# Feed-forward of a two-layer kernel: how many up products go with one step of the sigmoid pass, and where the up half is rounded first

## The chip, the cores and the metric

The kernel runs on one core of a Trainium2 chip. The metric is the time of one execution on the device in microseconds (us), taken as the median of several runs; lower is better. The engines are called as in the profile: PE (TensorE, matrix products), DVE (VectorE), ACT (ScalarE), POOL (GpSimd) and SP (SyncE, which here only issues DMAs). Each runs its own instructions strictly in the order in which they were written, and they wait for one another through semaphores.

## The reference, cut to what matters

4096 tokens of width 256 go through two mixture-of-experts layers, an attention and a feed-forward. The change touches the last one alone:

```python
x    = act_qdq(layernorm(x))                    # act_qdq: round to 16 bits with ONE scale for
up   = act_qdq(x @ lpbq_dequant(w_up).T)        # the whole tensor, scale = max|x| / 32767
gate = act_qdq(x @ lpbq_dequant(w_gate).T)
sig  = fixed_qdq_u16(jax.nn.sigmoid(gate))
gate = act_qdq(gate * sig)
o    = act_qdq(gate * up)
return o @ lpbq_dequant(w_down).T               # added to x
```

`gate`, `up` and `o` are 4096 x 768. Every `act_qdq` needs the largest absolute value of the whole tensor before the first element can be rounded, so each is a barrier between two passes over the data.

## The kernel before, in words

In `gated_ffn` the 4096 x 768 values of `gate` stay in SBUF (`act_all`, 128 partitions x 24,576 floats). `up` has no room there: it is made in 48 products of 128 x 512 (`NP` = 48), copied out of PSUM into one of four buffers `u_out` (`UB` = 4), and stored to the DRAM tensor `up_raw`. Later it is loaded back in 12 pieces of 128 x 2048 floats, 1 MB each, into `later`, which has four places (`LB` = 4) and lies in the memory of `yT`, the transposed input of the up products. So no piece can be loaded before the last up product.

Three stages matter here.

**Sigmoid pass**, 24 steps (`STEPS`) of 1024 columns. For step i, ACT rounds the gate values of step i+1 (`round_gate`, L1672), takes the sigmoid of step i (`sigmoid`, L1678) and copies two up products out of PSUM (`evict_up`, L1640). DVE makes the sigmoid's integers (`sigmoid_integers`, L1827), takes the largest gated value of the step before (`gated_max`, L1836), multiplies gate and sigmoid (`gated`, L1831), and takes the largest value of the same two up products (L1845). PE makes the up products; product n waits until product n-4 has left its bank. `evict_up(n)` waits for product n, for the store and the maximum of n-4 (its buffer). `sigmoid(i)` waits for `gated(i-4)`. SP issues the 48 stores (L1503), waits for all of them, and then issues the loads of the pieces (L1510).

**Two scales.** When the pass is over DVE reduces the 48 maxima of up (L1847), POOL reduces them over the partitions (L1528), and DVE computes the scale of up (`new_scale`, L1772 to L1777; semaphore `s_scale` becomes 3). The scale of the gated values follows in the same way (L1853; `s_scale` 4).

**Wide pass**, 12 pieces (`WIDE`). ACT rounds piece i of up in its place in `later` (`round_up`, L1691, waits for the load of piece i) and piece i of the gated values (`round_gated`, L1695). DVE multiplies the two (L1866) and takes the largest value of the product of the piece before (L1861). SP issues the load of piece i only when `s_o["product"]` has reached i-3, that is after the DVE product of piece i-4, which reads the same place:

```python
free(sp, s_o["product"], i - LB + 1)
sp.dma_start(later[:, i % LB, :], up_raw[:, i * CW:(i + 1) * CW]).then_inc(s_later[i % LB], 16)
```

The order of the instructions on each engine is the order of the Python loops; nothing reorders it. After the wide pass comes the down projection, which the change does not touch.

Of the kernel before, what the change touches and what calls it, by code (L numbers as in the profile page):

```python
# [9 lines left out]
ALU = mybir.AluOpType  # L10
ACT = mybir.ActivationFunctionType
AX_X = mybir.AxisListType.X
# [1352 lines left out]
def low16(ap):  # L1365

    return ap.bitcast(I16).rearrange("p (n two) -> p n two", two=2)[:, :, 0]


def gated_ffn(nc, name, x_all, stats, act_all, I, w_up, w_down, up_raw, out):  # L1370
# [16 lines left out]
    WIDE = COLS // CW  # L1387
    NP = TG * IC
    BANKS = 4
    UB = 4  # L1390
    PAIRS = T // 2
    SIG_ROUND = 192.0
    SIG_TOP = 65535.0 / 65536.0

    with ExitStack() as ctx:
        sem = ctx.enter_context(stage_semaphores(nc, name))

        def sb(n, shape, dt):
            return ctx.enter_context(nc.sbuf_tensor(f"{name}_{n}", shape, dt))
# [16 lines left out]
        round_c = sb("round_c", [P, 1], F32)  # L1416
# [8 lines left out]
        maxes = sb("maxes", [P, 2, NP], F32)  # L1425
        step_max = sb("step_max", [P, T], F32)
        largest = sb("largest", [P, 5], F32)
        reduced = sb("reduced", [P, 5], F32)

        scale = sb("scale", [P, 5], F32)  # L1430
        to_int = sb("to_int", [P, 5], F32)
        tmp = sb("tmp", [P, 5], F32)
        unit = sb("unit", [P, 3], F32)
        u_all = sb("u_all", [P, UB, N], F32)
        u_out = [u_all[:, p, :] for p in range(UB)]
        work = sb("work", [P, 4, CB], F32)
# [6 lines left out]
        later = yT[:].rearrange("p h c t -> p (h c t)").bitcast(F32).rearrange("p (n c) -> p n c", c=CW)  # L1443
        LB = 4
# [8 lines left out]
        s_big = sem("largest_ready"); s_red = sem("largest_reduced"); s_scale = sem("scales_ready")  # L1453
        s_t = sem("x_rounded"); s_qt = sem("x_transposed"); s_qh = sem("yT_hi_ready"); s_ql = sem("yT_lo_ready")
        s_pr = sem("product_in_bank"); s_ev = sem("bank_copied"); s_um = sem("up_max_taken")
        s_us = [sem(f"up{i}_stored") for i in range(UB)]
        s_g = {k: sem("gate_" + k) for k in ("rounded", "sigmoid", "sig", "product", "max")}
        s_later = [sem(f"later{i}_loaded") for i in range(LB)]
        s_o = {k: sem("o_" + k) for k in ("up_rounded", "rounded", "product")}
# [5 lines left out]
        BIG_X, BIG_GATE, BIG_UP, BIG_GATED, BIG_O = range(5)  # L1465
# [14 lines left out]

        def gate_at(g, c):
            return flat[:, g * GW + c * N:g * GW + (c + 1) * N]

        def step(i):
            return flat[:, i * CB:(i + 1) * CB]
# [12 lines left out]
        def _(sp):  # L1498
            sp.dma_start(w_in[1].rearrange("p (c d) -> p c d", d=D), w_up.rearrange("(c p) d -> p c d", p=P)).then_inc(s_w[1], 16)
            sp.dma_start(w_in[2].rearrange("p (c i) -> p c i", i=I), w_down.rearrange("(c p) i -> p c i", p=P)).then_inc(s_w[2], 16)  # L1500
            for n in range(NP):
                sp.wait_ge(s_ev, NP + n + 1)
                sp.dma_start(up_raw[:, n * N:(n + 1) * N], u_out[n % UB]).then_inc(s_us[n % UB], 16)  # L1503
            for b in range(UB):
                sp.wait_ge(s_us[b], 16 * (NP // UB))
            sp.wait_ge(s_pr, 2 * NP)
# [4 lines left out]
            out_pairs = out.rearrange("(q k p) d -> q p k d", k=2, p=P)  # L1511
            for q in range(PAIRS):
                sp.wait_ge(s_d["out"], q + 1)
                sp.dma_start(out_pairs[q], u_out[q % 2].rearrange("p (k d) -> p k d", k=2)).then_inc(s_out[q % 2], 16)
            for p in range(2):
                sp.wait_ge(s_out[p], 16 * PAIRS // 2)

# [14 lines left out]
        def _(pe):  # L1532
# [25 lines left out]
            def product(i, g, c0):  # L1558

                n = i * NP + g * IC + c0  # L1560
                if n >= BANKS:
                    pe.wait_ge(s_ev, n - BANKS + 1)
                y_at_g = [y[:, :, g * N:(g + 1) * N] for y in (yT_hi, yT_lo)]
                bank = ps[4 + n % BANKS][:]
                for c in range(DC):
                    hi, lo = (w[:, i, c, c0 * P:(c0 + 1) * P] for w in (guT_hi, guT_lo))
                    nc.tensor.matmul(bank, hi, y_at_g[0][:, c], start=(c == 0), stop=False)  # L1567
                    nc.tensor.matmul(bank, hi, y_at_g[1][:, c], start=False, stop=False)  # L1568
                    mm = nc.tensor.matmul(bank, lo, y_at_g[0][:, c], start=False, stop=(c == DC - 1))  # L1569
                mm.then_inc(s_pr, 1)  # L1570
# [15 lines left out]
            for g in range(TG):  # L1586
                for c0 in range(IC):
                    product(1, g, c0)
            for q in range(PAIRS):
                pe.wait_ge(s_d["lo"], q + 1)  # L1590
# [14 lines left out]
        def _(act):  # L1605
            A = nc.scalar
# [22 lines left out]
            def evict_gate(g, c0):  # L1629
                n = g * IC + c0  # L1630
                act.wait_ge(s_pr, n + 1)
                A.activation(gate_at(g, c0), ps[4 + n % BANKS][:], ACT.Copy).then_inc(s_ev, 1)

            def evict_up(n):
                act.wait_ge(s_pr, NP + n + 1)

                if n >= UB:
                    act.wait_ge(s_us[n % UB], 16 * (n // UB))
                    act.wait_ge(s_um, n - UB + 1)
                A.activation(u_out[n % UB], ps[4 + (NP + n) % BANKS][:], ACT.Copy).then_inc(s_ev, 1)  # L1640
# [13 lines left out]
            for g in range(TG):  # L1654
# [3 lines left out]
                for c0 in range(IC):  # L1658

                    if c0 == 0 and (g + 1) * GW > y_at and g * GW <= y_at + T * D:  # L1660
                        act.wait_ge(s_qt, min(PAIRS, 2 * g + 2))
                    evict_gate(g, c0)
# [8 lines left out]
            def round_gate(i):  # L1671
                A.activation(step(i), step(i), ACT.Identity, bias=round_c[:], scale=to_int[:, 1:2]).then_inc(s_g["rounded"], 1)  # L1672

            def sigmoid(i):
                act.wait_ge(s_g["rounded"], i + 1)
                if i >= SB:
                    act.wait_ge(s_g["product"], i - SB + 1)
                A.activation(sig[i % SB], low16(step(i)), ACT.Sigmoid, scale=scale[:, 1:2]).then_inc(s_g["sigmoid"], 1)  # L1678

            act.wait_ge(s_scale, 2)  # L1680
            round_gate(0)
            for i in range(STEPS):
                if i + 1 < STEPS:
                    round_gate(i + 1)
                sigmoid(i)
                for n in (2 * i, 2 * i + 1):
                    evict_up(n)

            def round_up(i):
                act.wait_ge(s_later[i % LB], 16 * (i // LB + 1))  # L1690
                A.activation(later[:, i % LB, :], later[:, i % LB, :], ACT.Identity, bias=round_c[:],  # L1691
                             scale=to_int[:, 2:3]).then_inc(s_o["up_rounded"], 1)

            def round_gated(i):
                A.activation(wide_step(i), wide_step(i), ACT.Identity, bias=round_c[:], scale=to_int[:, 3:4]).then_inc(s_o["rounded"], 1)  # L1695

            act.wait_ge(s_scale, 3)
            round_up(0)
            act.wait_ge(s_scale, 4)
            for i in range(WIDE):  # L1700
                round_gated(i)
                if i + 1 < WIDE:
                    round_up(i + 1)

            def round_product(q):

                if q >= 2:
                    act.wait_ge(s_d["lo"], q - 1)
                A.activation(wide[q % 2][:, 0:GW // 2].rearrange("p (c t) -> p c t", c=IC), pair_of_tiles(q),  # L1709
                             ACT.Identity, bias=round_c[:], scale=to_int[:, 4:5]).then_inc(s_d["rounded"], 1)  # L1710
# [9 lines left out]
            round_product(0)  # L1720
            for q in range(PAIRS):
                if q + 1 < PAIRS:
                    round_product(q + 1)
# [3 lines left out]
        def _(dve):  # L1727
            V = nc.vector
# [38 lines left out]
            def new_scale(c, unit):  # L1767


                big = reduced[:, c:c + 1]  # L1770
                if unit is not None:
                    order(V.tensor_scalar(tmp[:, c:c + 1], big, unit, None, ALU.mult))  # L1772
                    big = tmp[:, c:c + 1]
                order(V.tensor_scalar(scale[:, c:c + 1], big, 1 / QMAX, 1e-12, ALU.mult, ALU.max))
                order(V.reciprocal(to_int[:, c:c + 1], scale[:, c:c + 1]))
                if unit is not None:
                    order(V.tensor_scalar(to_int[:, c:c + 1], to_int[:, c:c + 1], unit, None, ALU.mult))  # L1777
# [28 lines left out]
            for g in range(TG):  # L1806
                for c0 in range(IC):
                    n = g * IC + c0
# [29 lines left out]
            for i in range(STEPS):  # L1838
                sigmoid_integers(i)
                if i > 0:  # L1840
                    gated_max(i - 1)
                gated(i)
                for n in (2 * i, 2 * i + 1):
                    dve.wait_ge(s_ev, NP + n + 1)
                    V.tensor_reduce(maxes[:, 1, n:n + 1], u_out[n % UB], AX_X, ALU.max, apply_absolute_value=True).then_inc(s_um, 1)  # L1845
            dve.wait_ge(s_um, NP)
            V.tensor_reduce(largest[:, BIG_UP:BIG_UP + 1], maxes[:, 1, :], AX_X, ALU.max).then_inc(s_big, 1)  # L1847
            gated_max(STEPS - 1)
            dve.wait_ge(s_red, 3)
            new_scale(2, unit[:, 0:1])  # L1850
            V.nop().then_inc(s_scale, 1)
            dve.wait_ge(s_g["max"], STEPS)
            V.tensor_reduce(largest[:, BIG_GATED:BIG_GATED + 1], step_max[:, 0:STEPS], AX_X, ALU.max).then_inc(s_big, 1)  # L1853
            dve.wait_ge(s_red, 4)
# [94 lines left out]
```

## Time and profile before

| | us |
|---|---|
| median of 3 runs (1688.80 to 1694.94) | 1692.29 |
| the profiled execution | 1692.64 |
| its span in the trace | 1690.9 |
| sigmoid pass, 1445.2 to 1542.9 | 97.7 |
| two scales, 1542.9 to 1548.0 | 5.1 |
| wide pass, 1548.0 to 1602.5 | 54.5 |
| down projection, 1602.5 to 1690.9 | 88.4 |

The span is what the trace covers; the profiled execution took 1.7 us more around it. Busy times of engines are not additive: the engines work beside one another. What bounds a stage is read from the engine that is never idle in it, and from what the others wait for.

### The profile page before, as it was taken

Reading aid. Unit: us, or ns where it says so; the run is one execution under the profiler, and the core shown is the slowest. Engines: PE = TensorE matmul, PEld = TensorE weight load, DVE = VectorE, ACT = ScalarE, POOL = GpSimd, SP = SyncE. Lnnn points to the kernel's source line nnn. Section 1 sums busy time; section 2 is a strip of 40 time slices with the busy share of each in tenths; the row PEclk is TensorE's granted clock in tenths of the full one; section 3 lists DMA queues with packets and bytes.
Section 4 is the critical chain, followed back from the end, with each engine's and each line's share of the span. In section 5 each row is a group of like instructions: output and inputs, shape, how many; then the busy total and the mean of one; then the engine's idle time right before and its main releaser. Section 6 shows DMA issues by size and latency. Waiting matters only on the chain. (4 is left out here: it accounts for less than half of the span.)

```text
span 1690.9 us, 31990 instructions
## 1 busy us (share of the span) xinstructions
PE 1317.8 (78%) x10558; PEld 1070.7 (63%) x10559; DVE 1198.5 (71%) x2040; ACT 832.3 (49%) x1240; POOL 523.8 (31%) x592
## 2 busy tenths in 40 slices
PE   6169999999999428999438898999998589761077
PEld 3159788888898217889426787878887545320066
DVE  3869766655565386976248888888888677898944
ACT  3447333333332225633116555555655456886764
POOL 0055666655653114565312223322224100000000
PEclk9579999999999668999758988888889589996599
DMA  9557433333232545732250000000000100336311
GB/s 326 157 155 223 98 51 54 50 50 47 47 48 26 184 136 168 227 60 43 28 169 11 10 10 9 9 9 9 9 9 4 38 1 1 125 124 225 122 45 57
DMA packets 103445, 134.31 MB, mean 79 GB/s; under 512 B 16192, under 2 KB 87488, under 8 KB 101568
## 3 DMA queue, kind: packets, MB, share of 16 engines
q1 hardware_dynamic: 81856, 103.33, 18.6%
q0 software_dynamic: 21504, 29.83, 10.8%
q8 instruction: 55, 0.90, 0.2%
q14 instruction: 30, 0.25, 0.0%
HBM read 88.43 MB, written 44.70 MB: 79 GB/s over the span
## 5 line engine op out<-in xcount | busy, mean ns | idle before, releaser
L600 ACT ACTIVATE top_x_all<-top_h_ps,top_b1T 128x256 f32<-128x256 f32 x448 | 186.3, 473 | 324.0 <-PE top_h_ps L480 278.5
L478 PE MATMUL top_h_ps<-top_xT_hi,top_w_hi 128*128 128x256 f16 x896 | 247.6, 276 | 1.9 <-DVE top_xT_lo L779 1.0
L479 PE MATMUL top_h_ps<-top_xT_lo,top_w_hi 128*128 128x256 f16 x896 | 247.6, 276 | 0.0
L480 PE MATMUL top_h_ps<-top_xT_hi,top_w_lo 128*128 128x256 f16 x896 | 247.4, 276 | 0.0
L496 PE MATMUL top_y_ps<-top_w_hi,top_x_all 128*128 x896 | 245.0, 273 | 0.1
L497 PE MATMUL top_y_ps<-top_w_lo,top_x_all 128*128 x896 | 244.9, 273 | 0.0
L498 PE MATMUL top_y_ps<-top_w_hi,top_x_all 128*128 x896 | 244.7, 273 | 0.0
L358 POOL DMA_INDIRECT x_sum<-top_x_all,top_rows_out x112 | 186.4, 1664 | 126.0 <-POOL top_rows_out L354 73.0
L790 DVE CAST top_x_all<-top_x_all 128x512 f16<-128x512 f32 x224 | 101.1, 451 | 150.9 <-ACT top_x_all L600 138.6
L792 DVE TENSOR_TENSOR top_x_all<-top_x_all 128x512 f16<-128x512 f32 x224 | 155.7, 695 | 7.7
L346 POOL DMA_INDIRECT top_xg<-normed,top_rows_in x112 | 123.2, 1100 | 90.1 <-POOL top_rows_in L343 81.7
L343 POOL COPY top_rows_in<-top_row_of_slot 128x1 int32<-128x1 int32 (+1 forms) x112 | 95.5, 852 | 133.2 <-DVE top_row_of_slot L769 133.0
L1113 PEld LDWEIGHTS attn_out_ps<-attn_v,attn_probT 128*128 128x128 f32 x1024 | 129.8, 202 | 4.7 <-issue 0.3
L1012 POOL TENSOR_TENSOR attn_q_parts<-attn_q,attn_q_parts 128x512 f16<-128x512 f32 x32 | 37.1, 1160 | 305.1 <-ACT attn_q_parts L1176 305.1
L1113 PE MATMUL attn_out_ps<-attn_v,attn_probT 128*128 128x17 f32 x1024 | 127.8, 267 | 0.0
L1599 PE MATMUL ffn_ps<-ffn_dT_hi,ffn_yT 128*128 128x256 f16 x192 | 53.1, 277 | 91.9 <-DVE ffn_yT L1879 91.9
L1103 PE MATMUL attn_S<-attn_ident,attn_prob 128*128 128x128 f32 x512 | 87.2, 325 | 37.1 <-ACT attn_prob L1192 37.0
L1196 ACT ACTIVATE attn_probT<-attn_S 128x1024 f32<-128x1024 f32 x64 | 65.5, 1024 | 83.4 <-PE attn_S L1103 83.4
L1311 DVE COPY_PREDICATED attn_S<-attn_masked,attn_tiny 128x1024 f32<-128x1024 int32 x64 | 103.5, 1617 | 1.7 <-PE attn_S L1097 1.6
L478 PEld LDWEIGHTS top_h_ps<-top_xT_hi,top_w_hi 128*128 x896 | 88.9, 99 | 13.3 <-issue 2.7
L1103 PEld LDWEIGHTS attn_S<-attn_ident,attn_prob 128*128 128x128 f32 x512 | 67.6, 163 | 46.4 <-ACT attn_prob L1192 43.3
L480 PEld LDWEIGHTS top_h_ps<-top_xT_hi,top_w_lo 128*128 x896 | 88.9, 99 | 11.3
(297 smaller groups left out, 3152.6 us busy)
## 6 DMA issues: line engine op xcount, KB each, us to landing
top_staged<-in_L_xattn_W SPq DMA_DIRECT2D x32, 512.0 KB
top_staged<-in_L_ffn_w SPq DMA_DIRECT2D x32, 512.0 KB
up_raw<-ffn_u_all SPq DMA_DIRECT2D x48, 256.0 KB, 2.1
ffn_yT<-up_raw SPq DMA_DIRECT2D x12, 1024.0 KB, 4.8
normed<-top_x_all SPq DMA_DIRECT2D x2, 4096.0 KB, 14.1
top_w_lo<-in_ctx SPq DMA_DIRECT2D x4, 1024.0 KB, 9.9
top_x_all<-in_x SPq DMA_DIRECT2D x4, 1024.0 KB, 11.8
x_sum<-top_x_all SPq DMA_DIRECT2D x4, 1024.0 KB, 11.1
```

What stands on the lines that cost most here:

```text
L346: nc.gpsimd.indirect_dma_start(out=xg[i][:, k, :], out_offset=None, in_=normed, in_offset=bass.IndirectOffsetOnAxis(ap=rows[:, 0:1], axis= ...
L358: nc.gpsimd.indirect_dma_start(out=x_sum, out_offset=bass.IndirectOffsetOnAxis(ap=rows_out[k][:, 0:1], axis=0), in_=y[p][:, k, :], in_offs ...
L478: nc.tensor.matmul(out, hi, xT_hi[p][:, c, :], start=(c == 0), stop=False)
L479: nc.tensor.matmul(out, hi, xT_lo[p][:, c, :], start=False, stop=False)
L480: last = nc.tensor.matmul(out, lo, xT_hi[p][:, c, :], start=False, stop=(c == DC - 1))
L496: nc.tensor.matmul(out, h_hi[p][:, fc, rows], hi, start=(fc == 0 and k == 0), stop=False, skip_group_check=True)
L497: nc.tensor.matmul(out, h_hi[p][:, fc, rows], lo, start=False, stop=False, skip_group_check=True)
L498: last = nc.tensor.matmul(out, h_lo[p][:, fc, rows], hi, start=False, stop=(fc == FC - 1), skip_group_check=True)
L600: last = nc.scalar.activation(h32[:, fc * R:(fc + 1) * R], h_ps[:, b, q * R:(q + 1) * R], ACT.Relu, bias=b1T[:, bass.ds(e * FC + fc, 1)], ...
L792: V.tensor_tensor(lo, part, hi, ALU.subtract).then_inc(s_hl[p], 1)
L1103: mm = nc.tensor.transpose(S[:, r, c, :], prob[:, r * HC + c, :], ident[:])
L1113: mm = nc.tensor.matmul(out_ps[:, h * V1:(h + 1) * V1], probT[:, h, :], v32[i][:, 2 * c + r, :], start=True, stop=True)
```

## The change

Three things are moved; no operation is added or taken away.

1. Three up products go with each of the first 16 steps of the sigmoid pass (`UP_STEPS` = 16) instead of two with each of the 24, on ACT and on DVE.
2. The reduction of up's maxima stands on DVE in step 16 and its scale in step 17.
3. ACT rounds the first four pieces of up (`round_up(0)` to `round_up(3)`) inside steps 19 to 22 of the sigmoid pass. In the wide pass `round_gated(i)` is then followed by `round_up(i + 4)` where it was followed by `round_up(i + 1)`.

SP's code is the same: 48 stores, then 12 loads with the same waits.

```diff
+    UP_A_STEP = 3
+    UP_STEPS = NP // UP_A_STEP
+    UP_EARLY = (UP_STEPS + 3, UP_STEPS + 4, UP_STEPS + 5, UP_STEPS + 6)
...
+        def ups(i):
+            return range(UP_A_STEP * i, min(NP, UP_A_STEP * (i + 1)))
...
             for i in range(STEPS):
                 if i + 1 < STEPS:
                     round_gate(i + 1)
                 sigmoid(i)
-                for n in (2 * i, 2 * i + 1):
+                for n in ups(i):
                     evict_up(n)
+                if i in UP_EARLY:
+                    act.wait_ge(s_scale, 3)
+                    round_up(i - UP_EARLY[0])
...
-            act.wait_ge(s_scale, 3)
-            round_up(0)
             act.wait_ge(s_scale, 4)
             for i in range(WIDE):
                 round_gated(i)
-                if i + 1 < WIDE:
-                    round_up(i + 1)
+                if i + LB < WIDE:
+                    round_up(i + LB)
...
                 gated(i)
-                for n in (2 * i, 2 * i + 1):
+                if i == UP_STEPS:
+                    dve.wait_ge(s_um, NP)
+                    V.tensor_reduce(largest[:, BIG_UP:BIG_UP + 1], maxes[:, 1, :], AX_X, ALU.max).then_inc(s_big, 1)
+                if i == UP_STEPS + 1:
+                    dve.wait_ge(s_red, 3)
+                    new_scale(2, unit[:, 0:1])
+                    V.nop().then_inc(s_scale, 1)
+                for n in ups(i):
...
-            dve.wait_ge(s_um, NP)
-            V.tensor_reduce(largest[:, BIG_UP:BIG_UP + 1], maxes[:, 1, :], AX_X, ALU.max).then_inc(s_big, 1)
             gated_max(STEPS - 1)
-            dve.wait_ge(s_red, 3)
-            new_scale(2, unit[:, 0:1])
-            V.nop().then_inc(s_scale, 1)
```

ACT's rows around the end of the sigmoid pass before the change (a row is a line of the program, the operation, what it writes and reads; L1678 is the sigmoid of the last steps, L1691 rounds a piece of up in the place of `yT`, L1695 a piece of the gated values):

```order
L1678 ACTIVATE ffn_work<-ffn_act_all,ffn_scale 128x1024
L1640 ACTIVATE ffn_u_all<-ffn_ps 128x512 x2
L1691 ACTIVATE ffn_yT<-ffn_yT,ffn_round_c,ffn_to_int 128x2048
L1695 ACTIVATE ffn_act_all<-ffn_act_all,ffn_round_c,ffn_to_int 128x2048
L1691 ACTIVATE ffn_yT<-ffn_yT,ffn_round_c,ffn_to_int 128x2048
L1695 ACTIVATE ffn_act_all<-ffn_act_all,ffn_round_c,ffn_to_int 128x2048
```

The same place after it, from step 22 on (L1678 is now `round_gate`, L1684 the sigmoid, L1688 rounds a piece of up, L1704 a piece of the gated values):

```order
L1678 ACTIVATE ffn_act_all<-ffn_act_all,ffn_round_c,ffn_to_int 128x1024
L1684 ACTIVATE ffn_work<-ffn_act_all,ffn_scale 128x1024
L1688 ACTIVATE ffn_yT<-ffn_yT,ffn_round_c,ffn_to_int 128x2048
L1684 ACTIVATE ffn_work<-ffn_act_all,ffn_scale 128x1024
L1704 ACTIVATE ffn_act_all<-ffn_act_all,ffn_round_c,ffn_to_int 128x2048
L1688 ACTIVATE ffn_yT<-ffn_yT,ffn_round_c,ffn_to_int 128x2048
L1704 ACTIVATE ffn_act_all<-ffn_act_all,ffn_round_c,ffn_to_int 128x2048
```

The kinds alternate in the wide pass as before, but the L1688 behind the first L1704 is now piece 4, where it was piece 1.

DVE's rows in steps 17 and 18 after the change (L1834, L1843 and L1838 are the three instructions of a step, L1779 to L1784 the scale of up):

```order
L1838 TENSOR_TENSOR ffn_act_all<-ffn_act_all,ffn_work 128x1024
L1779 TENSOR_SCALAR ffn_tmp<-ffn_reduced,ffn_unit 128x1
L1781 TENSOR_SCALAR ffn_scale<-ffn_tmp 128x1
L1782 RECIPROCAL ffn_to_int<-ffn_scale 128x1
L1784 TENSOR_SCALAR ffn_to_int<-ffn_to_int,ffn_unit 128x1
L1834 TENSOR_SCALAR ffn_work<-ffn_work 128x1024
```

The scale of up has moved in front of step 18; from there on a step has no maxima of up.

## Rows read from the trace of the kernel before

**Rows 1.** The page's first line.

```profile
span 1690.9 us, 31990 instructions
```

**Rows 2.** Busy time by stretch (count), then granted clock, DMA share, GB/s.

```profile
core 0: us, PE busy (x) PEld busy (x) DVE busy (x) ACT busy (x) POOL busy (x), PEclk, DMA share, GB/s
1445.20:1542.90 97.70, 60.80 (x264) 24.03 (x264) 97.54 (x122) 75.92 (x93) 0.35 (x1) 0.94 0.41 151
1548.00:1602.50 54.50, 0.00 (x0) 0.00 (x0) 52.88 (x24) 43.57 (x22) 0.00 (x0) 0.50 0.45 154
```

**Rows 3.** Groups by line, 1440 to 1545: busy, mean ns, idle before, releaser.

```profile
L1567 PE MATMUL ffn_ps<-ffn_yT,ffn_guT_hi 128*128 128x512 f16 x94 | 35.9, 381 | 23.3 <-ACT ffn_u_all L1640 23.3
L1640 ACT ACTIVATE ffn_u_all<-ffn_ps 128x512 f32<-128x512 f32 x48 | 28.0, 601 | 13.1 <-DVE ffn_maxes L1845 13.1
```

**Rows 4.** Timeline of DVE, one step: start, duration.

```profile
1533.41 0.68 DVE L1827 TENSOR_SCALAR ffn_work<-ffn_work 128x1024 f32<-128x1024 f32 x1
1534.01 1.21 DVE L1836 TENSOR_REDUCE ffn_step_max<-ffn_act_all 128x1 f32<-128x1024 f32 x1
1535.14 1.22 DVE L1831 TENSOR_TENSOR ffn_act_all<-ffn_act_all,ffn_work 128x1024 f32<-128x1024 int16 x1
1536.27 1.27 DVE L1845 TENSOR_REDUCE ffn_maxes<-ffn_u_all 128x1 f32<-128x512 f32 x2
1537.46 0.68 DVE L1827 TENSOR_SCALAR ffn_work<-ffn_work 128x1024 f32<-128x1024 f32 x1
```

**Rows 5.** Timeline of ACT, one step, with the idle time before.

```profile
1492.51 1.19 ACT L1640 ACTIVATE ffn_u_all<-ffn_ps 128x512 f32<-128x512 f32 x2 [0.69 <-DVE ffn_maxes L1845]
1493.60 1.23 ACT L1672 ACTIVATE ffn_act_all<-ffn_act_all,ffn_round_c,ffn_to_int 128x1024 f32<-128x1024 f32 x1
1494.73 1.14 ACT L1678 ACTIVATE ffn_work<-ffn_act_all,ffn_scale 128x1024 f32<-128x1024 int16 x1
```

**Rows 6.** Timeline of PE, two matmuls of an up product in a row.

```profile
1527.30 0.38 PE L1569 MATMUL ffn_ps<-ffn_yT,ffn_guT_lo 128*128 128x512 f16 x1
1527.52 0.38 PE L1567 MATMUL ffn_ps<-ffn_yT,ffn_guT_hi 128*128 128x512 f16 x1
```

**Rows 7.** Timeline of DVE, the two scales.

```profile
1542.87 0.20 DVE L1772 TENSOR_SCALAR ffn_tmp<-ffn_reduced,ffn_unit 128x1 f32<-128x1 f32 x1
...
1543.86 0.18 DVE L1853 TENSOR_REDUCE ffn_largest<-ffn_step_max 128x1 f32<-128x24 f32 x1
...
1545.15 0.21 DVE L1777 TENSOR_SCALAR ffn_to_int<-ffn_to_int,ffn_unit 128x1 f32<-128x1 f32 x1
```

**Rows 8.** Timeline of ACT, start of the wide pass.

```profile
1545.80 2.08 ACT L1695 ACTIVATE ffn_act_all<-ffn_act_all,ffn_round_c,ffn_to_int 128x2048 f32<-128x2048 f32 x1
1547.79 2.08 ACT L1691 ACTIVATE ffn_yT<-ffn_yT,ffn_round_c,ffn_to_int 128x2048 f32<-128x2048 f32 x1
1549.77 2.08 ACT L1695 ACTIVATE ffn_act_all<-ffn_act_all,ffn_round_c,ffn_to_int 128x2048 f32<-128x2048 f32 x1
```

**Rows 9.** Timeline of DVE, start and end of the wide pass.

```profile
1547.98 2.29 DVE L1866 TENSOR_TENSOR ffn_act_all<-ffn_act_all,ffn_yT 128x2048 f32<-128x2048 int16 x1 [2.31 <-ACT ffn_act_all L1695]
1551.88 2.29 DVE L1866 TENSOR_TENSOR ffn_act_all<-ffn_act_all,ffn_yT 128x2048 f32<-128x2048 int16 x1 [1.61 <-ACT ffn_act_all L1695]
1554.09 2.28 DVE L1861 TENSOR_REDUCE ffn_step_max<-ffn_act_all 128x1 f32<-128x2048 f32 x1
...
1598.04 4.47 DVE L1861 TENSOR_REDUCE ffn_step_max<-ffn_act_all 128x1 f32<-128x2048 f32 x2
```

**Rows 10.** The loads: one issue, SP's waits for DVE, and time to landing.

```profile
1550.30 0.32 SPq L1510 DMA_DIRECT2D ffn_yT<-up_raw  x1
...
SPq L1510 <- DVE ffn_act_all L1866: 39.8, 8, 11.8
...
DMA to landing us min/median/max: 4.7/4.8/11.4
```

**Rows 11.** Busy time by stretch, while the first four loads run together.

```profile
1539.00:1543.00 4.00, 0.00 (x0) 0.00 (x0) 3.96 (x7) 0.00 (x0) 0.35 (x1) 0.50 1.01 426
```

More of the change, by code:

```diff
@@ L1678, in sigmoid, with round_up @@
                 A.activation(sig[i % SB], low16(step(i)), ACT.Sigmoid, scale=scale[:, 1:2]).then_inc(s_g["sigmoid"], 1)
+            def round_up(i):
+                act.wait_ge(s_later[i % LB], 16 * (i // LB + 1))
+                A.activation(later[:, i % LB, :], later[:, i % LB, :], ACT.Identity, bias=round_c[:],
+                             scale=to_int[:, 2:3]).then_inc(s_o["up_rounded"], 1)
             act.wait_ge(s_scale, 2)
@@ L1685, in _ @@
                 sigmoid(i)
-                for n in (2 * i, 2 * i + 1):
+                for n in ups(i):
                     evict_up(n)
[L1689 to L1692, printed above, removed]
+                if i in UP_EARLY:
+                    act.wait_ge(s_scale, 3)
+                    round_up(i - UP_EARLY[0])
             def round_gated(i):
                 A.activation(wide_step(i), wide_step(i), ACT.Identity, bias=round_c[:], scale=to_int[:, 3:4]).then_inc(s_o["rounded"], 1)
-            act.wait_ge(s_scale, 3)
-            round_up(0)
             act.wait_ge(s_scale, 4)
```

## The prediction

> **What bounds the kernel now.** I read four views in this order. First the table of busy time by stretch: in the sigmoid pass DVE is busy 97.54 of 97.70 us and ACT 75.92, in the wide pass DVE 52.88 of 54.50 and ACT 43.57 [rows 2]. So DVE bounds both passes and the other engines have room. Second the groups by line, for who waits for whom: ACT's copies of up products waited 13.1 us for the maxima on DVE, and PE 23.3 us for ACT's copies [rows 3]. The chain of waits in the sigmoid pass ends on DVE. Third the timelines of DVE and ACT for the length of a step [rows 4, 5] and for the handover between the passes [rows 7 to 9]. Last SP's own waits and the times to landing, because the change moves ACT's roundings of up, and these wait for loads [rows 10].
>
> **Three up products a step.** On DVE a step with two maxima takes 1537.46 - 1533.41 = 4.05 us, of which the two maxima are 1537.46 - 1536.27 = 1.19 [rows 4]; the rest is 2.86 and one maximum is 0.60. With the change 16 steps take 2.86 + 3 x 0.60 = 4.65 and eight take 2.86: 74.4 + 22.9 = 97.3, against 24 x 4.05 = 97.2. DVE does the same work and gains nothing by it. The others must still fit under 4.65 us. ACT: two copies 1.09, rounding 1.13, sigmoid 1.14 by its duration [rows 5]; a third copy makes it 1.64 + 2.27 = 3.9. PE: matmuls start 0.22 us apart [rows 6], six a product, 18 a step, so 3.9. Both fit with 0.7 to spare, and the four buffers do not bind: a copy waits for the maximum of four products earlier, which ACT already meets by waiting 0.69 us a step [rows 5], and that wait only shrinks. I book this part at 0.
>
> **Scale of up inside the pass.** The four instructions of a scale take 1543.86 - 1542.87 = 0.99 us on DVE [rows 7]. They are moved, not removed, so DVE ends its pass when it did. POOL's reduction over partitions then lies beside step 17. Booked at 0. Counted back from the reduction of the gated maxima at 1543.86 [rows 7], one closing maximum of 1.13 [rows 4] and six steps of 2.86 before it, step 18 begins at 1543.86 - 1.13 - 17.16 = 1525.57, and the scale is there then.
>
> **First roundings inside the last steps.** In steps 19 to 22 ACT has rounding and sigmoid, some 2.2, and a piece of up, 1.99 from start to start [rows 8]: 4.2 us against DVE's 2.86. ACT has run ahead before, but each piece waits for the scale of up, so it starts this stretch at 1525.6. The sigmoid of step 22 stands behind three pieces: 1525.6 + 2 x 4.2 + 2.0 + 2.2 = 1538.2. DVE wants it at 1525.57 + 4 x 2.86 = 1537.0. That is a stall of 1.2; the last sigmoid adds about 0.2. ACT, hidden so far, is the bound here for 1.4 us. The loads of these pieces are in time: the last copy of up now comes near 1514, and four loads together, 4.2 MB at the 426 GB/s of [rows 11], need 10 us. In the old kernel the gated rounding could start when the second scale was ready, at 1545.15 + 0.21 = 1545.36 [rows 7], but ACT was busy with piece 0 of up until 1545.80 [rows 8]. Now it starts at 1545.36 + 1.4 = 1546.7, so the wide pass starts 0.9 us late, although a piece of up is out of its way.
>
> **The wide pass.** Here the change costs. ACT works strictly in order: `round_gated(i)`, then `round_up(i+4)`, then `round_gated(i+1)`. `round_up(i+4)` waits for the load of piece i+4. SP issues that load only after the DVE product of piece i, whose place in `later` it overwrites. And that product waits for `round_gated(i)`, which ACT has just done. So each load has no lead at all, and `round_gated(i+1)`, queued behind the waiting `round_up`, holds up DVE. Before, the load of piece 4 was issued at 1550.30, right as product 0 ended (1547.98 + 2.29) [rows 9, 10], and ACT needed it only three ACT pairs later; all eight such loads waited for DVE, 39.8 us in all [rows 10], and nobody waited for them. One round of the new loop:
> - start of the gated rounding to start of the product, 1551.88 - 1549.77 = 2.11 [rows 8, 9]
> - start of the product to issue of the load, 1550.30 - 1547.98 = 2.32 [rows 9, 10]
> - issue to landing, 4.8 (4.7 at least) [rows 10]
> - waking ACT, 0.10, as between ACT's end at 1547.88 and DVE's start at 1547.98 [rows 8, 9]
> - rounding of up to the next gated rounding, 1549.77 - 1547.79 = 1.98 [rows 8]
>
> The sum is 11.3 us, and there are eight rounds, i = 0 to 7: 90.4. From 1546.7 this leads to the gated rounding of piece 8 at 1637.1. Four products and five maxima (7 to 11) are left on DVE: 2.2 + 9 x 2.2 + 0.1 makes 1659.2. The wide pass ended at 1598.04 + 4.47 = 1602.51 [rows 9]. The difference is 56.7 us.
>
> The unknown in this is the lone load. Most of the old ones were in flight nearly alone (one each 4.4 us), which is why I take 4.8. From below it cannot be less than its bytes at full rate, 1.05 MB / 426 GB/s = 2.5 us [rows 11]: eight rounds of 9.0, so 18 us less. From above stands 11.4, the longest landing [rows 10], of four loads that queued behind each other: 53 us more. Neither end fits a single load, so they stay outside the range's core.
>
> The Trainium skill, page "DMA: Bandwidth & Descriptors", section "Anatomy of one DMA — SWDGE (gpsimd) path", gives a DMA some 2.0 us of fixed cost plus its bytes at 436 GB/s. For 1 MB that is an estimate of 4.4 us, and the sum would be 3 us smaller, near 1746; the trace's 4.8 is of the same transfer, so it decides. Its section "Rules for kernel authors" says to issue a DMA early and wait for it late, which is what this change undoes: the old trace shows the rule kept, with no wait of ACT for a load.
>
> After the wide pass nothing changes. PE is idle through the wide pass in both, at a granted clock of 0.50, half of 2.4 GHz [rows 2], so the down projection starts as cold as before.
>
> **Sum.** The profiled execution took 1692.64 us for a span of 1690.9 [rows 1], 0.35 above the median 1692.29 of the runs. 1692.64 + 56.7 is 1749.3; the smallest landing, 4.7, gives 0.8 less. I predict 1749.
>
> **Rivals.**
> A, no slower: the loads keep their lead. If a load were issued before its turn on ACT, the wide pass would stay bound by DVE, with its old gap between the first two products. Then only the start moves: +0.9, so 1693.5, or, if ACT also kept up in steps 19 to 22, 1545.36 - 1545.80 = -0.4, so 1692.2. It decides from the point where a load leaves 4.8 us before ACT reaches `round_up(i+4)`. For it speaks that the old loads were always in time; against it that SP's wait for the product of i is unchanged and cannot be met sooner. Likewise it needs ACT to take the next `round_gated` past a waiting rounding, which no in-order engine does.
> B, the loop is there but the load lands faster because nothing else is in the queues: at 2.5 us, 1731. Against it: the minimum of twelve landings is 4.7.
> C, much slower: PE falls to its lower clock, 1.2 GHz, in the sigmoid pass. A step's three products would take 2 x 3.9 = 7.8 us against 4.65, in 16 steps 50 us on top: 1799. Against it: the granted clock of that stretch is 0.94, tail without matmuls included [rows 2], and PE gets busier, not idler.
> D, DVE or ACT is slowed by the early loads, which now run beside full steps: not in the trace, since the old first four loads ran beside DVE at 3.96 of 4.00 busy [rows 11]. A few us at most, inside the range.
>
> **Chances.** Forecast 0.91; A 0.04 (of this 0.01 faster by over 0.3%), B 0.03, C 0.02. The range, 1742 to 1757, covers the forecast with landings of 4.3 to 5.2 us (8 x 0.45 = 3.6 each way) and the spread of 6 us between runs. About 0.3%, 5 us, is what a measurement here can tell from no change. Faster 0.01, same 0.03, slower 0.96.
>
> **What would show it.** In the new profile: DVE steps of 4.65 us up to 1518 and of 2.86 after, with about 1 us of idle time before steps 22 and 23 released by ACT's sigmoid; ACT's first pieces of up from 1525.6 on; in the wide pass eight products 11.3 us apart, then DVE without a gap; ACT idle some 7 us (9.3 from the gated rounding's start, less its 2.08) before a `round_up`, released by a DMA, eight times, and PE idle for about 57 us longer before the down projection. I am wrong if products in the wide pass stay 4.4 us apart, if ACT's waits for a load fall well below 7 us, or if a step with three up products takes over 5 us.

## The result, and the profile after

| | median, us | runs |
|---|---|---|
| before | 1693.62 | 6, from 1688.80 to 1699.76 |
| changed | 1748.76 | 6, from 1743.92 to 1752.99 |

The ratio is 1.0325, 95% interval 1.0298 to 1.0352: the change makes the kernel 55 us slower. The prediction was 1749, between 1742 and 1757.

The profiled execution of the changed kernel took 1752.99 us. The whole program in front of the feed-forward is the same, yet its sigmoid pass begins 3.6 us later (1448.87 against 1445.29), so the traces are best compared by distances inside the feed-forward. I use one distance throughout: from DVE's first instruction of the sigmoid pass to the reduction that closes the wide pass. Before it is 1602.54 - 1445.29 = 157.25 us, after it 1662.78 - 1448.87 = 213.91. The two marks before the change, and the first one after it (the closing one stands further down):

```profile
1445.29 0.69 DVE L1827 TENSOR_SCALAR ffn_work<-ffn_work 128x1024 f32<-128x1024 f32 x1 [4.73 <-ACT ffn_work L1678]
...
1602.54 0.17 DVE L1871 TENSOR_REDUCE ffn_largest<-ffn_step_max 128x1 f32<-128x12 f32 x1
```

```profile
1448.87 0.69 DVE L1834 TENSOR_SCALAR ffn_work<-ffn_work 128x1024 f32<-128x1024 f32 x1 [4.73 <-ACT ffn_work L1684]
```

First the busy times by stretch, the same columns as in [rows 2]: the sigmoid pass with its scales, then the wide pass.

```profile
1448.80:1550.40 101.60, 59.94 (x264) 24.06 (x264) 99.42 (x130) 82.89 (x97) 1.07 (x2) 0.84 0.44 166
1552.60:1662.70 110.10, 0.00 (x0) 0.00 (x0) 53.51 (x24) 38.57 (x19) 0.00 (x0) 0.50 0.23 76
```

DVE does the same 53 us of work in the wide pass, but in 110.1 us instead of 54.5. ACT is less busy than before, and the DMA engines too (0.23 against 0.45). All three idle half the time or more: no engine bounds this stage, a loop through all of them does. The granted clock of 0.84 in the first row is not a slower PE: from 1448.87 to 1520, where the up products are made, it is 0.98, and in the 30 us after the last of them, with PE idle, 0.50. Who waits for whom from 1440 to 1670 (us in total, times, longest):

```profile
DVE ffn_act_all L1875 <- ACT ffn_act_all L1704: 58.6, 9, 8.8
ACT ffn_yT L1688 <- DMA ffn_yT<-up_raw: 57.7, 8, 7.6
...
ACT ffn_u_all L1646 <- DVE ffn_maxes L1859: 10.3, 13, 0.8
PE ffn_ps L1573 <- ACT ffn_u_all L1646: 6.3, 11, 1.5
```

DVE waits for ACT and ACT for the loads, eight times each with one more at the start for DVE. The two waits are the same 57 us or so seen twice, not 116. The first round of the loop, DVE first (with product 8 and the closing reduction further on), then ACT, then SP's issue of a load in it:

```profile
1552.59 2.29 DVE L1875 TENSOR_TENSOR ffn_act_all<-ffn_act_all,ffn_yT 128x2048 f32<-128x2048 int16 x1 [1.97 <-ACT ffn_act_all L1704]
1563.66 2.29 DVE L1875 TENSOR_TENSOR ffn_act_all<-ffn_act_all,ffn_yT 128x2048 f32<-128x2048 int16 x1 [8.78 <-ACT ffn_act_all L1704]
...
1642.88 2.29 DVE L1875 TENSOR_TENSOR ffn_act_all<-ffn_act_all,ffn_yT 128x2048 f32<-128x2048 int16 x1 [6.76 <-ACT ffn_act_all L1704]
...
1662.78 0.17 DVE L1880 TENSOR_REDUCE ffn_largest<-ffn_step_max 128x1 f32<-128x12 f32 x1
```

```profile
1550.40 2.09 ACT L1704 ACTIVATE ffn_act_all<-ffn_act_all,ffn_round_c,ffn_to_int 128x2048 f32<-128x2048 f32 x1 [5.87 <-DVEq L1865]
1559.56 2.09 ACT L1688 ACTIVATE ffn_yT<-ffn_yT,ffn_round_c,ffn_to_int 128x2048 f32<-128x2048 f32 x1 [7.06 <-DMA ffn_yT<-up_raw]
1561.55 2.08 ACT L1704 ACTIVATE ffn_act_all<-ffn_act_all,ffn_round_c,ffn_to_int 128x2048 f32<-128x2048 f32 x1
```

```profile
1554.91 0.32 SPq L1516 DMA_DIRECT2D ffn_yT<-up_raw  x1
```

Read it as a circle: gated rounding of piece 0 at 1550.40, product at 1552.59, load of piece 4 issued at 1554.91, the rounding of piece 4 at 1559.56, gated rounding of piece 1 at 1561.55. Before, the product of piece 1 came 3.9 us after that of piece 0 [rows 9]; now 11.1. Products 0 and 8 are 90.29 us apart, 11.29 a piece.

In the sigmoid pass the steps have the lengths that were worked out: a step with three up products takes 1522.17 - 1517.53 = 4.64 us, one without 1537.58 - 1534.71 = 2.87. The only new stall is where ACT's sigmoid is late. Step 21 begins at 1537.58, step 22 at 1541.54 and step 23 at 1544.57:

```profile
1517.53 0.67 DVE L1834 TENSOR_SCALAR ffn_work<-ffn_work 128x1024 f32<-128x1024 f32 x1
...
1522.17 0.67 DVE L1834 TENSOR_SCALAR ffn_work<-ffn_work 128x1024 f32<-128x1024 f32 x1
...
1534.71 0.69 DVE L1834 TENSOR_SCALAR ffn_work<-ffn_work 128x1024 f32<-128x1024 f32 x1
...
1537.58 0.69 DVE L1834 TENSOR_SCALAR ffn_work<-ffn_work 128x1024 f32<-128x1024 f32 x1
...
1541.54 0.69 DVE L1834 TENSOR_SCALAR ffn_work<-ffn_work 128x1024 f32<-128x1024 f32 x1 [1.02 <-ACT ffn_work L1684]
...
1544.57 0.69 DVE L1834 TENSOR_SCALAR ffn_work<-ffn_work 128x1024 f32<-128x1024 f32 x1
```

From the closing reduction to the end of the span it is 88.4 us before and after: the down projection did not change.

### The profile page after: what moved, and what is told of

It is laid out like the page before. It is cut to its first block and busy times, and to the rows that moved or that the text cites. A ratio compares the mean times of both kernels' runs of the same rounds, so it can differ in the third digit from the quotient of the medians.

```text
span 1751.2 us, 31993 instructions
## 1 busy us (share of the span) xinstructions
PE 1318.3 (75%) x10558; PEld 1072.2 (61%) x10559; DVE 1200.1 (69%) x2040; ACT 830.7 (47%) x1240; POOL 526.0 (30%) x592
## 5 line engine op out<-in xcount | busy, mean ns | idle before, releaser
L358 POOL DMA_INDIRECT x_sum<-top_x_all,top_rows_out x112 | 187.1, 1670 | 125.4 <-POOL top_rows_out L354 77.3
L1605 PEld LDWEIGHTS ffn_ps<-ffn_dT_hi,ffn_yT 128*128 128x128 f16 x192 | 19.1, 99 | 172.3 <-DVE ffn_yT L1888 169.9
L1103 PE MATMUL attn_S<-attn_ident,attn_prob 128*128 128x128 f32 x512 | 93.9, 343 | 37.8 <-ACT attn_prob L1192 37.8
L1103 PEld LDWEIGHTS attn_S<-attn_ident,attn_prob 128*128 128x128 f32 x512 | 73.7, 173 | 47.0 <-ACT attn_prob L1192 43.6
```

Of the source, the lines that this page charges most:

```text
L358: nc.gpsimd.indirect_dma_start(out=x_sum, out_offset=bass.IndirectOffsetOnAxis(ap=rows_out[k][:, 0:1], axis=0), in_=y[p][:, k, :], in_offs ...
L1103: mm = nc.tensor.transpose(S[:, r, c, :], prob[:, r * HC + c, :], ident[:])
```

## The experiments

Each kernel is a small edit away from the kernel before or from the changed one. The column "distance" is the one defined above, from each kernel's own trace, one execution each. The times are medians where no "one run" stands beside them, and the ratios are to runs of the kernel before that were made together with them.

| kernel | distance, us | against before | time, us |
|---|---|---|---|
| before | 157.25 | | 1693.62; the traced execution 1692.64 |
| changed | 213.91 | +56.66 | 1748.76; the traced execution 1752.99 |
| three products a step only | 157.13 | -0.12 | 1694.48; ratio 0.9994 (0.9976 to 1.0013) |
| two ahead | 156.72 | -0.53 | 1694.23; ratio 1.0004 (0.9992 to 1.0016) |
| one ahead | 168.58 | +11.33 | 1702.67, one run |
| half loads | 203.82 | +46.57 | 1742.56, one run |
| scale early, no early roundings | 157.02 | -0.23 | 1691.70, one run |
| stock of two | 157.02 | -0.23 | 1691.50, one run |
| no stall | 155.59 | -1.66 | 1691.19; ratio 0.9982 (0.9965 to 0.9998) |
| before with the new wide order | 218.27 | +61.02 | 1755.37, one run |

**Three products a step only**

```diff
+    UP_A_STEP = 3
...
-                for n in (2 * i, 2 * i + 1):
+                for n in range(UP_A_STEP * i, min(NP, UP_A_STEP * (i + 1))):
```

The loop head is changed on ACT and on DVE.

> The first part alone: three up products with each of the first 16 steps of the sigmoid pass; scales, first roundings and the order of the wide pass as in the kernel before. My theory: DVE does the same work, steps are 4.65 us and then 2.86, nobody else becomes the bound; the time stays within 0.3% of the kernel before, the wide pass ends within 0.2 us of where it did (measured from the start of the sigmoid pass), ratio 1.000. Rival: three products a step overload PE, ACT or the four buffers, and this part carries a share of the 56 us: a step then takes over 5 us and the kernel is slower by at least 16 x 0.35 = 6 us.

The ratio is 0.9994 (0.9976 to 1.0013). A step with three products is 4.65 us on DVE, here with start and duration:

```profile
1515.67 0.68 DVE L1828 TENSOR_SCALAR ffn_work<-ffn_work 128x1024 f32<-128x1024 f32 x1
...
1518.54 1.86 DVE L1846 TENSOR_REDUCE ffn_maxes<-ffn_u_all 128x1 f32<-128x512 f32 x3
1520.32 0.68 DVE L1828 TENSOR_SCALAR ffn_work<-ffn_work 128x1024 f32<-128x1024 f32 x1
```

This part costs nothing and gains nothing within the interval, which allows some 4 us faster and 2 us slower. The rival of an overloaded PE, ACT or buffer, with at least 6 us, is out.

**Two ahead**

```diff
             for i in range(WIDE):
                 round_gated(i)
-                if i + LB < WIDE:
-                    round_up(i + LB)
+                if i >= 2 and i - 2 + LB < WIDE:
+                    round_up(i - 2 + LB)
```

> The changed kernel with one edit in the wide pass: ACT rounds gated pieces 0, 1 and 2 before the first round_up, so that round_up(i+2) stands behind round_gated(i) and its load has two more pieces of lead. Loads, waits and early roundings are those of the changed kernel. My theory (the 57 us are a load without lead, in a loop with two roundings and a product): a load, 4.8, with the two roundings and product is one round of 11.3 us for three pieces, 3.8 a piece, less than DVE's 4.4. So all is hidden, DVE runs through its 24 instructions without a gap of 1.6, and the wide pass ends 0.6 us before that of the kernel before: about 1692, ratio to before 0.999 to 1.001. Rival (early loads, three products a step or the early roundings cost something themselves): most of the 57 us stays.

The ratio to the kernel before is 1.0004 (0.9992 to 1.0016), and the distance is 0.53 us shorter than before, where 0.6 had been expected: two places' difference in the order of ACT's instructions gives back the whole loss. Everything else of the change is still in this kernel, the early loads, the four early roundings and the stall in steps 22 and 23 among it. So the loss lies in the order of ACT in the wide pass. Of the waits for loads 3.8 us are left, and DVE's wait is only that for the first gated rounding:

```profile
ACT ffn_yT L1688 <- DMA ffn_yT<-up_raw: 3.8, 3, 3.1
DVE ffn_act_all L1875 <- ACT ffn_act_all L1704: 2.0, 1, 2.0
```

**One ahead**

```diff
-                if i + LB < WIDE:
-                    round_up(i + LB)
+                if i >= 1 and i - 1 + LB < WIDE:
+                    round_up(i - 1 + LB)
```

> The same edit with one piece of lead: round_up(i+3) stands behind round_gated(i). My theory in numbers: two pieces share a round of 11.3 us, 5.65 a piece against 4.4, products come in pairs 4.4 and 6.9 us apart, and the wide pass ends 11.2 us later than in the kernel before, so some 1704 us in one run. Rival (the loads land slower or faster by where they are issued, or there is a fixed penalty for each): anything not near half of 11.3 us a piece.

The distance is 11.33 us longer than before, against 11.2 expected. The products come in pairs, as they must if two pieces share one round; DVE's timeline:

```profile
1547.73 4.49 DVE L1875 TENSOR_TENSOR ffn_act_all<-ffn_act_all,ffn_yT 128x2048 f32<-128x2048 int16 x2 [1.98 <-ACT ffn_act_all L1704]
...
1558.85 2.29 DVE L1875 TENSOR_TENSOR ffn_act_all<-ffn_act_all,ffn_yT 128x2048 f32<-128x2048 int16 x1 [4.43 <-ACT ffn_act_all L1704]
...
1563.25 2.28 DVE L1875 TENSOR_TENSOR ffn_act_all<-ffn_act_all,ffn_yT 128x2048 f32<-128x2048 int16 x1
...
1570.04 2.29 DVE L1875 TENSOR_TENSOR ffn_act_all<-ffn_act_all,ffn_yT 128x2048 f32<-128x2048 int16 x1 [2.31 <-ACT ffn_act_all L1704]
```

From 1558.85 to 1563.25 are 4.4 us, DVE's own pace; to the next pair 6.8, where 6.9 had been expected. With none, one and two pieces of lead a piece takes 11.3, 5.6 and 4.4 us: the round divided by one, by two, and, where a third of it (3.8) is less than DVE's work, DVE's work.

**Half loads**

```diff
-                sp.dma_start(later[:, i % LB, :], up_raw[:, i * CW:(i + 1) * CW])...
+                part = CW if i < LB else CW // 2
+                sp.dma_start(later[:, i % LB, 0:part], up_raw[:, i * CW:i * CW + part])...
```

> The changed kernel, but the loads of pieces 4 to 11 bring only the first 1024 of their 2048 columns (0.5 MB); the other half of a place keeps older values, so the output differs. All waits and all compute instructions stay. My theory: landing is a fixed part and the bytes at some 430 GB/s, so it falls from 4.8 to 3.6 us, a round from 11.3 to 10.1, and the kernel is 8 x 1.2 = 10 us faster than the changed one, about 1739. Rival 1: landing is all bytes: 2.4 us, 19 us faster. Rival 2: it is all latency: no change.

Against the changed kernel the distance shrinks by 213.91 - 203.82 = 10.1 us, 1.26 a round; 10 had been expected. Time from issue to landing in the wide pass, minimum, median and maximum, first of the changed kernel, then of this one:

```profile
DMA to landing us min/median/max: 4.6/4.8/5.2
```

```profile
DMA to landing us min/median/max: 3.4/3.5/3.9
```

Half the bytes take off 1.3 us of 4.8. Both rivals, all bytes and all latency, are out. If the time grows evenly with the bytes, which two sizes cannot show, an estimate from them is 2.6 us for the bytes (1.05 MB at some 400 GB/s) and 2.2 for a fixed part.

**Scale early, no early roundings.** Parts one and two of the change with the old wide pass.

```diff
-    UP_EARLY = (UP_STEPS + 3, UP_STEPS + 4, UP_STEPS + 5, UP_STEPS + 6)
+    UP_EARLY = ()
...
+            act.wait_ge(s_scale, 3)
+            round_up(0)
             act.wait_ge(s_scale, 4)
             for i in range(WIDE):
                 round_gated(i)
-                if i + LB < WIDE:
-                    round_up(i + LB)
+                if i + 1 < WIDE:
+                    round_up(i + 1)
```

> Parts one and two of the change without the third: three up products a step, the scale of up in steps 16 and 17, but no early roundings (only piece 0 before the wide pass) and the wide pass in the old order, round_up(i+1) behind round_gated(i). My theory: ACT rounds piece 0 of up while DVE ends its pass, so the gated rounding starts when the second scale is ready, 0.4 us earlier than before, and everything after it is as before: wide pass 0.4 us earlier, some 1692. Rival (the early scale or the early loads disturb the pass): the sigmoid pass gets longer than 97.7 us by a microsecond or more.

The distance is 0.23 us shorter than before; 0.4 had been expected. The gated rounding begins 1544.77 - 1444.51 = 100.26 us into the distance, where it was 1545.80 - 1445.29 = 100.51 [rows 8]. The reduction of the gated maxima, with which the sigmoid pass ends, comes 98.66 us into the distance, where it was 98.57: the early loads and the early scale cost less than 0.1 us, not the microsecond or more of the rival.

**Stock of two**

```diff
-    UP_EARLY = (UP_STEPS + 3, UP_STEPS + 4, UP_STEPS + 5, UP_STEPS + 6)
+    UP_EARLY = (UP_STEPS + 3, UP_STEPS + 4)
...
-                if i + LB < WIDE:
-                    round_up(i + LB)
+                if i + 2 < WIDE:
+                    round_up(i + 2)
```

> The changed kernel with only two early pieces (in steps 19 and 20) and round_up(i+2) behind round_gated(i): each load is issued two products before ACT needs it, as deep a lead as in the two-ahead kernel, reached with fewer pieces in stock. My theory: what counts is the distance between a load's issue and its rounding, not how many pieces are ready: a round of 11.3 us for three pieces is hidden behind DVE's 4.4 each, no stall in the last steps of the sigmoid pass, wide pass ends 0.4 us before that of the kernel before, some 1692. Rival (the early roundings themselves cost): still slower than before.

The distance is 0.23 us shorter than before, where 0.4 had been expected, and 56.9 shorter than that of the changed kernel, which has four pieces in stock. The early roundings themselves do not cost it, and the two-ahead kernel has all four of them: what counts is how long before its rounding a load is issued. This version gets the lead by taking less in advance, the two-ahead version by running the gated roundings ahead; both hide the load.

**No stall.** The two-ahead kernel with pieces 2 and 3 of up behind the last sigmoid.

```diff
+    UP_EARLY = {UP_STEPS + 3: (0,), UP_STEPS + 4: (1,), STEPS - 1: (2, 3)}
...
                 if i in UP_EARLY:
                     act.wait_ge(s_scale, 3)
-                    round_up(i - UP_EARLY[0])
+                    for n in UP_EARLY[i]:
+                        round_up(n)
```

> The two-ahead kernel, with the early pieces of up placed so that they hold up no sigmoid: piece 0 in step 19, piece 1 in step 20, pieces 2 and 3 behind the last sigmoid. My theory: the 1.2 us that DVE waited for the sigmoids of steps 22 and 23 are gone, the wide pass starts when the second scale is ready and has no gap: it ends 1.9 us before that of the kernel before, some 1691 us, ratio 0.999, which is below what a measurement of times resolves but to be seen in the trace. Rival: ACT is late with pieces 2 and 3, and the gated rounding starts later than 1545.4 on the clock of the kernel before: no gain over the two-ahead kernel.

The ratio is 0.9982 (0.9965 to 0.9998), the distance 1.66 us shorter than before against 1.9 expected. The busy times of its wide pass, the same columns as in [rows 2]:

```profile
1549.10:1602.20 53.10, 0.00 (x0) 0.00 (x0) 52.92 (x24) 38.07 (x19) 0.00 (x0) 0.50 0.45 158
```

DVE is busy 52.92 of 53.10, so as long as DVE has this work, another order has nothing more to give in the wide pass; what this one gives is 1.7 us of 1692. It has the shortest distance of the kernels here, by an amount that the medians hardly resolve.

**Before with the new wide order**

```diff
             act.wait_ge(s_scale, 3)
-            round_up(0)
+            for i in range(LB):
+                round_up(i)
             act.wait_ge(s_scale, 4)
             for i in range(WIDE):
                 round_gated(i)
-                if i + 1 < WIDE:
-                    round_up(i + 1)
+                if i + LB < WIDE:
+                    round_up(i + LB)
```

> The kernel before with only the order of the roundings changed: pieces 0 to 3 of up are rounded one after the other when the scale of up is ready (after the sigmoid pass), and in the wide pass round_up(i+4) stands behind round_gated(i). Two products a step, the scale after the pass. My theory: the same loop of 11.3 us eight times, 55.8 us more than the old wide pass, and three more roundings of up (3 x 2.0) before its start: 61.7 us more, some 1754. Rival (the cost needs the shortened staging of up or the early scale): well under 50 us.

The distance is 61.02 us longer than before, 61.7 had been expected. ACT waits for the loads as in the changed kernel (us in total, times, longest):

```profile
ACT ffn_yT L1691 <- DMA ffn_yT<-up_raw: 57.2, 8, 7.3
```

Put into the old kernel, the order alone makes the loss; it needs nothing else of the change.

## Why the prediction was right, step by step

- **Three products a step, 0.** A step is 4.65 us with three maxima, as worked out from [rows 4]; the part alone moves the distance by -0.12.
- **Scale of up inside the pass, 0.** It was expected 80.3 us after the start of the pass (1525.6 - 1445.29). ACT's first piece of up starts at 1528.92, 80.05 after it. Without the early roundings the wide pass comes 0.23 earlier.
- **Stall in steps 22 and 23, 1.2 + 0.2.** From start to start step 21 takes 1541.54 - 1537.58 = 3.96 us instead of 2.86 and step 22 takes 1544.57 - 1541.54 = 3.03, so the stall is 1.10 + 0.17 = 1.27, and not 1.4. The gated rounding starts 1550.40 - 1448.87 = 101.53 us into the distance, 1.02 later than in [rows 8], where 0.9 was expected. Two misses in opposite directions lie behind this small one. The stall was sized 0.13 too long. And the working had the gated rounding start 1545.36 - 1543.86 = 1.50 us after the reduction of the gated maxima began, at an unchanged place; even without a stall, in the kernel with the early scale alone, that reduction comes 0.09 later, and the rounding 1.60 after it. There ACT already waits for the scale and has to be woken, for which the loop's sum has 0.10 and this one nothing.
- **The loop, eight rounds of 11.3.** Rounds take 11.29 on average. The parts of the first, which has the shortest landing, are 2.19 to the product (1550.40 to 1552.59), 2.32 to the issue (1554.91), 4.65 to the rounding of up (1559.56) and 1.99 to the next gated rounding, 11.15 together; from issue to rounding the eight rounds take 4.65 to 5.24. The landing, the unknown of the sum, was 4.8 in the median as in [rows 10]. The Trainium skill, page "DMA: Bandwidth & Descriptors", section "Anatomy of one DMA — SWDGE (gpsimd) path", gives a fixed part plus bytes for DMAs that POOL issues; here SP issues them. Its estimate for half a megabyte is 1.2 us, where the half loads show 1.3, and its estimate of 4.4 for the whole load is 0.4 less than the 4.8 measured. The 1746 that went with it was inside the range too, so the time of the whole kernel does not tell the two apart; the landings do.
- **The sum, 56.7.** The distance grew by 56.66. The median of 1748.76, a quarter of a microsecond from 1749, is closer than the method earns: the forecast started from one execution at 1692.64, the six runs before have a median of 1693.62, and runs of one kernel differ by 9 to 11 us. The medians are 55.1 us apart.
- **Rivals.** A, that the loads keep their lead, is nearly what the two-ahead kernel does: its distance is 0.53 shorter, which is A's later start of the pass (+1.0) less the old gap of 1.6 between the first two products [rows 9]. The changed kernel doesn't do so. B, a lone load at 2.5 us: the shortest was 4.6. C, PE at its lower clock: PE's matmuls stay 0.38 us long in the pass, at a granted clock of 0.98, and the steps 4.65. D, the early loads disturb DVE: the steps beside them and behind them keep their length, 2.87 us.
- **One sign was wrong.** PE was to be idle about 57 us longer before the down projection. From the last matmul of an up product to the first of the down projection it is idle 156.9 us, and 82.3 before: 75 longer. The other 18 us come from the up products being done earlier; the kernel with three products a step alone has them too (100.1). They cost nothing, since PE bounds neither stage.

The terms were each measured: the loop by three kernels that change its lead (one ahead, two ahead, stock of two), one that has the old order, one that puts the new order into the old kernel, and one that changes the load. What was not tried is a version with more than four places for pieces, since the memory of `yT` holds no more.

## What to carry to other kernels

Work taken in advance from a ring of buffers does not give the loads a lead. Here it took the lead away: with all four places full of finished work, the next load can start only when the consumer frees a place, and if the engine that frees it then stands in order behind the rounding of that very load, load, rounding and product follow one another. Before moving a step that waits for a load, write down for each load what frees its place, and count the instructions on the waiting engine between that event and the wait. In the kernels here the time per piece was the round divided by the lead in pieces plus one (11.3 and 5.6 us), or the busiest engine's work (4.4 us) where that was longer.

## What the runs showed of the hardware

The parts of the program ahead of the feed-forward are the same in all ten traces, yet the sigmoid pass starts anywhere from 1441.06 to 1448.87 us. Inside the feed-forward the expected distances came out within 0.7 us, and from the closing reduction to the end it is 88.4 us in nine traces and 89.05 in one. So most of the 8 to 15 us by which runs of a kernel differ probably comes from before the feed-forward; this is not shown, since there is one trace of each kernel. A distance between two marks of one trace told differences here that the medians of a dozen runs did not.

A load of 1 MB alone on the queues lands 4.6 to 5.2 us after its issue, one of 0.5 MB 3.4 to 3.9.
